# State sums of a Mamba block taken time-major: accumulating transposes, the skip term as a matmul, gated rows turned back in pairs

## The chip, the cores and the metric

The kernel runs on one core of a Trainium2 chip. The metric is the device time of one execution in microseconds (us). The kernel before was run three times: 1104.54 us median, 1101.55 to 1105.68. A further, profiled execution took 1106.44 us.

## What is computed

A decoder layer on x of 8 batches of 256 positions and 256 channels: a Mamba block (selective scan), cross attention with a feed-forward part, and a mixture of 160 experts, each behind a layer norm. The change lies in the Mamba block, whose end the reference writes so:

```
u = silu(conv(x_in)); dt, Bm, Cm = split(u @ x_proj_w.T)
delta = softplus(dt @ dt_proj_w.T + dt_proj_b)
h = h * exp(delta_t * A) + (delta_t * u_t) * b_t      # for each channel d and state n
y = einsum('bdn,bn->bd', h, c_t)                      # sum over 16 states
y = ys + u * D_param
y = y * silu(z)
out = y @ out_proj_w.T
```

There are 512 inner channels d, 16 states n and 256 time steps t per batch.

## The kernel before

Everything is float32 but for a few masks. Five engine programs, written out by hand, run side by side and meet by semaphores; the order of each engine's work is the order of the calls in its function `turn(s, p)`. Turn s works on four batches at once: the scan of batch s, the attention front of batch s-1, the feed-forward part of s-2, routing of s-3 and its scatter to DRAM (also of s-4), and the projections of batch s+1. Ten turns (-2 to 7), then a hand-made tail that finishes the last batches. Behind this front, which ends near 750 us, come the experts and a combining stage, which the change doesn't touch.

**The scan.** The 512 channels are 4 chunks c of 128 partitions, the 16 states 4 groups of 4. One of the 16 steps t of a batch takes one group and one chunk: ScalarE makes the decays in a PSUM tile DA (two of them; `decay`, L722 and four exponentials L725), GpSimd makes the inflow (three buffers; `inflow`, L462), VectorE scans (`scan`, L1668, 128x1024) and multiplies by C into one of four SBUF tiles hb (`outflow`, L1675). TensorE adds the four states of hb into the PSUM bank Y (`sum_`, L1123): four matmuls with the identity as weights and 256 columns of hb moving, so that Y holds channel by time. `inflow(t)` waits for scan t-2 to start and scan t-3 to end; `decay(t)` waits for outflow t-2.

**The gate.** After four steps a chunk is complete, and VectorE does `y(b, p, c)`: L1681 adds u * D to Y in PSUM, L1684 multiplies by silu(z) and writes the result over u. The four calls stand in VectorE's list after scan 5 (c = 0), scan 10 (c = 1), before scan 13 (c = 2), and after scan 1 of the next turn (c = 3). The first sum of the next chunk waits for `y` (y_d), since it overwrites Y. `out_proj` (L1135) takes the gated u as weights. It needs all four chunks and stands in the next turn, in bank QA.

**Around it.** `in_proj(b, 2)` and `in_proj(b, 3)` (L1087) make z, channel by time, copied to `sz` by ScalarE (`z_in`, L674). `conv_` (L1096) and `conv_out` (L667) are the convolution through bank PB and its bias. On VectorE the moments of a layer norm end in L1698; the root that GpSimd takes of them is L468 to L473 (`ln_root`). `ln0` follows scan 4, `ln1` stands just before y of c = 2. `router` on TensorE (L1248) is read by VectorE in L1741 at the head of the next turn. `acc` takes the shared expert's result (`shared_out`, L1753) and is stored to DRAM; `base2` (L499, GpSimd, `base2_`) is the feed-forward's residual, and GpSimd reaches it after `inflow` 5. In the tail, `out7(c)` (L1453) is the output projection of the last batch, and `ffn1_6` (L1549) stands between its pieces.

Of the kernel before, what the change touches and what calls it, by code (L numbers as in the profile page):

```python
# [80 lines left out]
def decoder_kernel(nc, a, out):  # L81
    ctx = ExitStack()
    with ctx:
# [24 lines left out]
        b_dt = sb("b_dt", [P, NC])  # L108
        a_neg = sb("a_neg", [P, NC, NS])
# [43 lines left out]
        k_scaled = sig("k_scaled")  # L153
# [21 lines left out]
        y_du = sig("y_du", NC)  # L175
# [64 lines left out]
        acc = sb("acc", [P, QT, D])  # L240
# [35 lines left out]
        full, used = xin[:, 0, 0:NE], xin[:, 1, 0:1]  # L276

# [151 lines left out]
        def front_gpsimd(pool):  # L429
# [65 lines left out]
            def base2_(b):  # L495
                pool.wait_ge(aff1_d.sem, aff1_d.at(b, 2))
                if ff_c.at(b - 1, 1, True):
                    pool.wait_ge(ff_c.sem, ff_c.at(b - 1, 1))
                g.tensor_tensor(base2[:, :, :], x2a[:, :, :], row(B2), ALU.add).then_inc(aff1_d.sem, 1)  # L499
# [150 lines left out]
        def front_scalar(act):  # L650
# [19 lines left out]
            def z_in(b, p, f):  # L670
                if f == 0 and y_d.at(b - 2, NC, True):
                    act.wait_ge(y_d.sem, y_d.at(b - 2, NC))
                act.wait_ge(proj_f.sem, proj_f.at(b, f + 5))
                s.activation(sz[p][:, 2 * f:2 * f + 2, :], pair(PB), ACT.Copy).then_inc(proj_c.sem, 1)  # L674
# [38 lines left out]
            def decay(b, p, t):  # L713
                gr, c = t % NG, t // NG
                if t == 0:
                    act.wait_ge(dl_d.sem, dl_d.at(b, 1))
                    if isinstance(b, int) and b == 0:
                        act.wait_ge(k_scaled.sem, 2)
# [91 lines left out]
            def first_batch():  # L810
                FB = [PB, QA]
                for f in range(2):
                    act.wait_ge(proj_f.sem, f + 1)
                    s.activation(xin[:, 2 * f:2 * f + 2, TAPS - 1:], pair(FB[f]), ACT.Copy).then_inc(proj_c.sem, 1)
                for f in range(2):
                    act.wait_ge(proj_f.sem, f + 3)
                    for i in range(2):
                        c = 2 * f + i
                        ins = s.activation(du[0][:, c, :], pair(FB[f])[:, i, :], ACT.Identity, bias=b_conv[:, c:c + 1])
                    ins.then_inc(proj_c.sem, 1)  # L820
                    act.wait_ge(proj_c.sem, f + 3)
# [18 lines left out]
                s.activation(sz[0][:, :, :], sz[0][:, :, :], ACT.Silu).then_inc(gate_d.sem, 1)  # L840

            first_batch()
            def turn(s, p):
# [5 lines left out]
                if exists(s + 1) and s >= 0:  # L849
                    conv_out(s + 1, 1 - p, 1)  # L850
                if exists(s) and s > 0:
                    decay(s, p, 3)
# [66 lines left out]
                if exists(s + 2) and s > -2:  # L919
                    x_in(s + 2, 0)  # L920
                if s == -1:
# [102 lines left out]
            def tail():  # L1024
                chosen_exp(L5)
                last_eps()
# [43 lines left out]
        def front_tensor(pe):  # L1070
            mm, tr = nc.tensor.matmul, nc.tensor.transpose

            def in_proj(b, f):
# [10 lines left out]
                for i in range(2):  # L1084
                    c = 2 * f + i
                    for k in range(KD):
                        ins = mm(pair(PB)[:, i, :], w_in[:, k, c * P:(c + 1) * P], xt[:, k, :],  # L1087
                                 start=k == 0, stop=k == KD - 1)
# [26 lines left out]

            def sum_(b, t):
                gr, c = t % NG, t // NG
                if gr == 0:
                    if y_d.at(b, c, True):
                        pe.wait_ge(y_d.sem, y_d.at(b, c))  # L1120
                pe.wait_ge(outflow_d.sem, outflow_d.at(b, t + 1))
                for n in range(SG):
                    ins = mm(Y[:, 0:T], ident[:, :], hb[t % NH][:, n, :],  # L1123
                             start=gr == 0 and n == 0, stop=gr == NG - 1 and n == SG - 1, skip_group_check=True)
                ins.then_inc(sum_d.sem, 1)

            def out_proj(b, p):
                pe.wait_ge(y_d.sem, y_d.at(b, NC))
                if acc_d.at(b - 2, 1, True):
                    pe.wait_ge(acc_d.sem, acc_d.at(b - 2, 1))  # L1130
                elif mg_c.at(b - 1, 1, True):
                    pe.wait_ge(mg_c.sem, mg_c.at(b - 1, 1))
# [107 lines left out]
            def x2T(b, p):  # L1240
                pe.wait_ge(norm_d[3].sem, norm_d[3].at(b, 1))
                turned(x2[p], QF, x2T_f)
# [70 lines left out]
            def first_batch():  # L1313
# [32 lines left out]
                for f in range(2):  # L1346
                    pe.wait_ge(proj_c.sem, f + 5)
                    projected(FB[1 - f], f + 2)

            first_batch()  # L1350
            def turn(s, p):
# [10 lines left out]
                if exists(s - 3):  # L1362
                    rank(s - 3)
                if exists(s):
                    sum_(s, 0)
                if exists(s - 1):
# [3 lines left out]
                if exists(s):  # L1370
                    sum_(s, 1)
# [12 lines left out]
                if exists(s):  # L1384
                    sum_(s, 4)
# [35 lines left out]
                if exists(s):  # L1421
                    sum_(s, 8)
# [12 lines left out]
                if exists(s):  # L1435
                    sum_(s, 12)
# [146 lines left out]
            def tail():  # L1583
# [5 lines left out]
                ffn1_6(0)  # L1589
                out7(2)  # L1590
# [43 lines left out]
        def front_vector(dve):  # L1634
# [10 lines left out]
            v.tensor_scalar(a_neg[:, :, :], a_neg[:, :, :], -1.0, None, ALU.mult).then_inc(k_scaled.sem, 2)  # L1645
# [934 lines left out]
```

## Time and profile before

| | us |
|---|---|
| profiled execution | 1106.44 |
| its span | 1104.7 |
| median of three runs | 1104.54 |
| TensorE busy (matmul) | 955.0 (86%) |
| VectorE busy | 838.1 (76%) |
| GpSimd busy | 746.9 (68%) |
| ScalarE busy | 631.5 (57%) |
| first scan of batch 0 starts | 43.07 |
| last step (outflow) of batch 7 starts | 652.43 |
| first matmul of the experts | 757.11 |

PE is TensorE's matmuls, PEld its weight loads, DVE VectorE, ACT ScalarE, POOL GpSimd, SP the engine that issues most transfers. L12 is line 12 of the kernel before. Busy time is what instructions cover; the shares are means over stages that differ, so the table alone doesn't say what bounds the scan. A matmul of float32 shows as two instructions in the trace where the program has one; a transpose shows as one.

### The profile page before, as it was taken

The page shows a single profiled execution, that of the slowest core. Times are in us where ns is not written, and L with a number is a line of the kernel's source. Part 1 is how long each engine was busy: PE and PEld are TensorE (multiplying, and loading weights), DVE is VectorE, ACT ScalarE, POOL GpSimd, SP SyncE. Part 2 cuts the span into 40 slices and gives each one's busy share as a digit, 9 for nine tenths or more (in the row PEclk, how much of TensorE's full clock was granted, in tenths as well). Part 3 has the DMA queues.
Part 4 walks back from the last instruction along what each step waited for, and adds up shares of the span by engine and source line. Part 5 has one row for each costly group of instructions (what it writes and reads, how often), then busy time and mean ns, then how long its engine had stood idle before and what let it go on. Part 6 is the DMA issues. An engine that isn't in the chain of part 4 may idle for free. (4 is left out here: it accounts for less than half of the span.)

```text
span 1104.7 us, 17544 instructions
## 1 busy us (share of the span) xinstructions
PE 955.0 (86%) x4878; PEld 799.0 (72%) x4878; DVE 838.1 (76%) x1640; ACT 631.5 (57%) x1560; POOL 746.9 (68%) x648
## 2 busy tenths in 40 slices
PE   6698979999999999999988989705999899999386
PEld 4476758788888888888866877605878787788264
DVE  0669999999999999999999984663655555555277
ACT  4776686785875876866855543403645455555200
POOL 1444585757679889888988886563777777777500
PEclk9698999999999999999989989967999999999799
DMA  7472764835115224224143112438998989988486
GB/s 241 172 244 91 233 197 153 262 106 172 41 35 179 77 64 150 72 96 142 39 142 96 43 61 74 160 111 273 328 305 261 293 287 284 295 277 258 157 341 265
DMA packets 118252, 195.46 MB, mean 177 GB/s; under 512 B 17476, under 2 KB 83170, under 8 KB 115714
## 3 DMA queue, kind: packets, MB, share of 16 engines
q1 hardware_dynamic: 79682, 134.54, 37.8%
q0 software_dynamic: 16512, 35.19, 8.7%
q10 hardware_dynamic: 21952, 24.51, 6.9%
q8 instruction: 42, 0.69, 0.3%
q14 instruction: 64, 0.52, 0.2%
HBM read 155.21 MB, written 75.64 MB: 209 GB/s over the span
## 5 line engine op out<-in xcount | busy, mean ns | idle before, releaser
L462 POOL TENSOR_TENSOR inf_all<-bc_all,du 128x1024 f32<-128x1024 f32 x128 | 300.6, 2367 | 97.0 <-DVEq L1666 48.5
L1668 DVE TENSOR_TENSOR_SCAN DA<-DA,inf_all 128x1024 f32<-128x1024 f32 x128 | 293.1, 2290 | 15.6 <-ACT DA L725 12.7
L2223 POOL DMA_INDIRECT yp_dram<-u,sz x216 | 212.9, 986 | 79.3 <-issue 41.7
L1123 PE MATMUL Y<-hb_all,ident 128*128 128x256 f32 x1024 | 247.3, 389 | 12.5 <-DVE u L1684 12.5
L1123 PEld LDWEIGHTS Y<-hb_all,ident 128*128 128x128 f32 x1024 | 197.2, 195 | 44.8 <-DVE u L1684 16.4
L725 ACT ACTIVATE DA<-dl,a_neg 128x255 f32<-128x255 f32 x512 | 211.9, 461 | 0.2
L2290 ACT ACTIVATE u<-DA,sz 128x256 f32<-128x256 f32 x216 | 102.6, 475 | 112.6 <-DMA yp_dram<-u,sz 79.6
L1675 DVE TENSOR_TENSOR hb_all<-DA,bc_all 128x1024 f32<-128x1024 f32 x128 | 155.8, 1218 | 8.2 <-DVE DA L1668 1.0
L2258 PE MATMUL DA<-hb_all,sz 128*128 128x256 f32 x432 | 136.6, 398 | 18.8 <-ACT sz L2283 17.7
L2251 PE MATMUL DA<-sz,hb_all 128*128 128x128 f32 x864 | 132.9, 277 | 2.9 <-issue 2.9
L2251 PEld LDWEIGHTS DA<-sz,hb_all 128*128 128x128 f32 x864 | 114.3, 193 | 3.7 <-issue 3.3
L2390 DVE COPY sz<-QA 128x256 f32<-128x256 f32 x108 | 45.8, 424 | 89.4 <-PE QA L2242 86.1
L515 POOL DMA_INDIRECT xe_dram<-x2e,ad_i x80 | 86.3, 1078 | 18.3 <-issue 17.1
L2258 PEld LDWEIGHTS DA<-hb_all,sz 128*128 128x128 f32 x432 | 65.5, 191 | 30.0 <-ACT sz L2283 28.4
L722 ACT ACTIVATE DA<-zeros 128x4 f32<-128x4 f32 x128 | 22.4, 175 | 104.3 <-DVE hb_all L1675 101.4
L2283 ACT ACTIVATE sz<-DA 128x128 f32<-128x128 f32 x216 | 59.1, 273 | 36.2 <-PE DA L2251 24.5
L1087 PE MATMUL PB<-xt,w_in 128*128 128x256 f32 x224 | 57.5, 402 | 16.8 <-DMA xt<-in_xT 9.5
L2242 PE MATMUL PB<-ident,inf_all 128*128 128x128 f32 x216 | 41.8, 276 | 34.8 <-DMA inf_all<-xe_dram 34.8
L2390 DVE COPY sz<-PB 128x256 f32<-128x256 f32 x108 | 45.8, 424 | 25.8 <-PE PB L2242 25.3
L2242 PEld LDWEIGHTS PB<-ident,inf_all 128*128 128x128 f32 x216 | 30.7, 143 | 45.8 <-DMA inf_all<-xe_dram 35.2
L1087 PEld LDWEIGHTS PB<-xt,w_in 128*128 128x128 f32 x224 | 43.8, 200 | 27.2 <-DMA xt<-in_xT 9.9
L1096 PE MATMUL PB<-xin,w_tap 128*128 128x256 f32 x224 | 51.1, 380 | 2.7 <-ACT du L667 2.0
(460 smaller groups left out, 1589.3 us busy)
## 6 DMA issues: line engine op xcount, KB each, us to landing
hb_all<-in_w_moe SPq DMA_DIRECT2D x216, 256.0 KB
bc_all<-bc_dram SPq DMA_DIRECT2D x32, 1024.0 KB, 5.9
inf_all<-xe_dram SPq DMA_DIRECT2D x216, 140.0 KB
bc_all<-yp_dram SPq DMA_DIRECT2D x16, 1024.0 KB, 6.9
xe_dram<-zeros ACTq DMA_DIRECT2D x2, 7420.0 KB, 26.0
xe_dram<-zeros ACTq DMA_DIRECT2D x1, 7560.0 KB, 27.1
yp_dram<-u,sz POOLq DMA_INDIRECT x216
xt<-in_xT SPq DMA_DIRECT2D x8, 256.0 KB, 5.8
```

What stands on the lines that cost most here:

```text
L462: g.tensor_tensor(inf[(b * NTAU + t) % NI][:, :, :], bc[gr][:, 0, :, :], du[p][:, c, :].unsqueeze(1).to_broadcast([P, SG, T]), ALU.mult).t ...
L515: g.indirect_dma_start(xe_dram, bass.IndirectOffsetOnAxis(ap=ad_i[b % 2][:, q, k:k + 1], axis=0), x2e[p][:, q, :].bitcast(I32), None).then ...
L725: ins = s.activation(da[:, n, 1:T], dl[p][:, c, 1:T], ACT.Exp, scale=a_neg[:, c, st:st + 1])
L1087: ins = mm(pair(PB)[:, i, :], w_in[:, k, c * P:(c + 1) * P], xt[:, k, :], start=k == 0, stop=k == KD - 1)
L1123: ins = mm(Y[:, 0:T], ident[:, :], hb[t % NH][:, n, :], start=gr == 0 and n == 0, stop=gr == NG - 1 and n == SG - 1, skip_group_check=True)
L1668: v.tensor_tensor_scan(da[:, :], da[:, :], inf[(b * NTAU + t) % NI][:, :, :].rearrange("p n t -> p (n t)"), 0.0, ALU.mult, ALU.add).then_i ...
L1675: v.tensor_tensor(hb[t % NH][:, :, :], states(DA[t % NDA]), bc[t % NG][:, 1, :, :], ALU.mult).then_inc(outflow_d.sem, 1)
L2223: g.indirect_dma_start(yp_dram, bass.IndirectOffsetOnAxis(ap=pid[:, half * UNROLL + s_:half * UNROLL + s_ + 1], axis=0), ys[s_][:, :], Non ...
L2251: ins = mm(UP[s_ % 2][:, 0:P], wt[s_][:, k * INTER:(k + 1) * INTER], xgT[s_ % 2][:, k, :], start=k == 0, stop=k == KD - 1)
L2258: mm(DN[s_ % 2][:, 0:D], h1[s_ % 2][:, :], wt[s_][:, KD * INTER:], start=True, stop=True).then_inc(dn_f.sem, 1)
L2290: s.activation(ys[s_][:, :], DN[s_ % 2][:, 0:D], ACT.Identity, scale=both[:, s_, 0:1]).then_inc(dn_c.sem, 1)
L2390: v.tensor_copy(xgT[s_ % 2][:, :, :], XT[s_ % 2][:, 0:KD * P].rearrange("p (k t) -> p k t", k=KD)).then_inc(xgT_c.sem, 1)
```

## The change

TensorE now builds Y time-major: two quarters of 128 time steps, each 128 partitions (time) by 128 columns (channels).

- `sum_`: each state of hb is the weights of two 128x128 transposes, with the identity moving, that accumulate in Y. Eight transposes take the place of four matmuls.
- `skip_`, new: u * D comes from two matmuls per chunk, u as weights and `d_tap` (a diagonal matrix of D, made once on ScalarE by four ACTIVATEs) moving. It opens the chunk's sum and has the wait for `y` of the chunk before.
- `y`: L1681 is gone. One VectorE multiply takes Y times silu(z) and writes over sz.
- z is projected time-major: two matmuls with 512 columns instead of four with 256, of the same columns in all.
- The gated rows have to be channel-major for `out_proj`. `gated_turned`, new, turns two chunks (four transposes), and `gated_out`, new, copies them from PSUM to u on ScalarE (128x512). Half 0 goes through bank QF late in the turn, half 1 through QA early in the next.
- `acc` and `base2` share one tile; `base2_` waits for the store of acc of the batch before. Sum 1 is moved ahead of `out_proj`.

```
 def in_proj(b, f):
...
+    else:
+        for k in range(KD):
+            ins = mm(PB[:, :], xt[:, k, rows_half(f - 2)], w_in[:, k, DI:], start=k == 0, stop=k == KD - 1)
+def skip_(b, p, c):
+    if y_d.at(b, c, True):
+        pe.wait_ge(y_d.sem, y_d.at(b, c))
+    else:
+        pe.wait_ge(a_exp.sem, 2)
+    for q in range(QT):
+        mm(YT[:, q, :], u[p][:, c, rows_half(q)], d_tap[:, c, :], start=q == 0, stop=False, skip_group_check=True)
 def sum_(b, t):
...
     for n in range(SG):
-        ins = mm(Y[:, 0:T], ident[:, :], hb[t % NH][:, n, :],
-                 start=gr == 0 and n == 0, stop=gr == NG - 1 and n == SG - 1, skip_group_check=True)
+        for q in range(QT):
+            ins = mm(YT[:, q, :], hb[t % NH][:, n, rows_half(q)], ident[:, :], is_transpose=True,
+                     start=False, stop=gr == NG - 1 and n == SG - 1, skip_group_check=True)
+def gated_turned(b, p, half, bank):
...
+    for i in range(2):
+        c = 2 * half + i
+        for q in range(QT):
+            ins = tr(pair(bank)[:, i, rows_half(q)], gated[p][:, q, c * P:(c + 1) * P], ident[:, :])
+    ins.then_inc(gT_f.sem, 1)
 def out_proj(b, p):
-    pe.wait_ge(y_d.sem, y_d.at(b, NC))
...
+    pe.wait_ge(gT_c.sem, gT_c.at(b, 2))
+def gated_out(b, p, half, bank):
+    act.wait_ge(gT_f.sem, gT_f.at(b, half + 1))
+    s.activation(u[p][:, 2 * half:2 * half + 2, :], pair(bank), ACT.Copy).then_inc(gT_c.sem, 1)
 def y(b, p, c):
     dve.wait_ge(gate_d.sem, gate_d.at(b, 1))
     dve.wait_ge(sum_d.sem, sum_d.at(b, NG * (c + 1)))
-    v.scalar_tensor_tensor(Y[:, 0:T], u[p][:, c, :], d_par[:, c:c + 1], Y[:, 0:T],
-                           ALU.mult, ALU.add).then_inc(y_du.sem, 1)
-    dve.wait_ge(y_du.sem, y_du.at(b, c + 1))
-    v.tensor_tensor(u[p][:, c, :], Y[:, 0:T], sz[p][:, c, :], ALU.mult).then_inc(y_d.sem, 1)
+    at = slice(c * P, (c + 1) * P)
+    v.tensor_tensor(gated[p][:, :, at], YT, gated[p][:, :, at], ALU.mult).then_inc(y_d.sem, 1)
 first_batch (ScalarE)
+    for c in range(NC):
+        ins = s.activation(d_tap[:, c, :], ident[:, :], ACT.Copy, scale=d_par[:, c:c + 1])
 tail (TensorE)
     ffn1_6(0)
+    gated_turned(L7, 1, 1, DA1[0])
     out7(2)
```

TensorE's list at the head of a steady turn, before (hs, ws_d: shared expert; w_tap: convolution; msk_b, m_sum: routing; w_out: output projection):

```order
L1264 MATMUL QA<-ws_d,hs 128x256 x2
L1096 MATMUL PB<-xin,w_tap 128x256 x8
L1123 MATMUL Y<-hb_all,ident 128x256 x4
L1087 MATMUL PB<-xt,w_in 128x256 x4
L1271 MATMUL QF<-msk_b,earlier 128x160
L1272 MATMUL QF<-m_sum,ones 128x160
L1273 MATMUL QF<-msk_b,earlier 128x160
L1274 MATMUL QF<-msk_b,ones 128x160
L1275 MATMUL QF<-m_sum,ones 128x160
L1123 MATMUL Y<-hb_all,ident 128x256 x4
L1135 MATMUL QA<-w_out,u 128x256 x8
L1087 MATMUL PB<-xt,w_in 128x256 x4
```

The same place in the changed kernel (L1151 the transposing sums, L1172 the turning back, L1144 the skip term):

```order
L1118 MATMUL PB<-xin,w_tap 128x256 x8
L1151 MATMUL Y<-ident,hb_all 128x128 x8
L1110 MATMUL PB<-w_in,xt 128x512 x2
L1316 MATMUL QF<-msk_b,earlier 128x160
L1317 MATMUL QF<-m_sum,ones 128x160
L1318 MATMUL QF<-msk_b,earlier 128x160
L1319 MATMUL QF<-msk_b,ones 128x160
L1320 MATMUL QF<-m_sum,ones 128x160
L1172 MATMUL QA<-ident,sz 128x128 x4
L1144 MATMUL Y<-d_tap,u 128x128 x2
L1151 MATMUL Y<-ident,hb_all 128x128 x16
L1179 MATMUL QA<-w_out,u 128x256 x8
```

The turning back and the skip term stand ahead of sums 0 and 1, and both sums ahead of the output projection.

ScalarE's list at the same place, before (L786 is the routing mask, L667 conv_out, then decay 3, z, decay 4):

```order
L786 ACTIVATE msk_b<-rep,m_half 128x320
L667 ACTIVATE du<-PB,b_conv 128x256 x2
L722 ACTIVATE DA<-zeros 128x4
L725 ACTIVATE DA<-dl,a_neg 128x255 x4
L674 ACTIVATE sz<-PB 128x512
```

and in the changed kernel:

```order
L796 ACTIVATE msk_b<-rep,m_half 128x320
L673 ACTIVATE du<-PB,b_conv 128x256 x2
L736 ACTIVATE u<-QA 128x512
L728 ACTIVATE DA<-zeros 128x4
L731 ACTIVATE DA<-dl,a_neg 128x255 x4
L680 ACTIVATE sz<-PB 128x512
```

The copy of half 1, L736, now stands between the convolution's bias and decay 3. The copy of half 0 stands in the same way between an x copy and decay 14.

## Rows read from the trace of the kernel before

**Rows 1.** Engines' busy time in two stretches; last columns clock, DMA share, GB/s.
```profile
100.00:280.00 180.00, 169.25 (x771) 140.95 (x770) 169.03 (x156) 123.23 (x294) 115.99 (x77) 0.99 0.56 178
280.00:550.00 270.00, 267.43 (x1255) 224.82 (x1254) 263.04 (x334) 200.90 (x470) 229.11 (x182) 1.00 0.28 92
```
**Rows 2.** VectorE's timeline: start, us covered; scan 6 of two turns, one y.
```profile
373.25 2.30 DVE L1668 TENSOR_TENSOR_SCAN DA<-DA,inf_all 128x1024 f32<-128x1024 f32 x1
...
429.48 0.47 DVE L1681 SCALAR_TENSOR_TENSOR Y<-u,d_par,Y 128x256 f32<-128x256 f32 x1
429.98 0.42 DVE L1684 TENSOR_TENSOR u<-Y,sz 128x256 f32<-128x256 f32 x1
...
451.78 2.30 DVE L1668 TENSOR_TENSOR_SCAN DA<-DA,inf_all 128x1024 f32<-128x1024 f32 x1
```
**Rows 3.** VectorE's waits from 100 to 280 us, and one in its timeline.
```profile
DVE DA L1668 <- ACT DA L725: 4.5, 6, 1.0
...
106.43 0.49 DVE L1681 SCALAR_TENSOR_TENSOR Y<-u,d_par,Y 128x256 f32<-128x256 f32 x1 [1.70 <-PE Y L1123]
```
**Rows 4.** TensorE's timeline: a sum's matmuls, four transposes, the next sum.
```profile
438.49 1.89 PE L1123 MATMUL Y<-hb_all,ident 128*128 128x256 f32 x8
440.22 0.60 PE L1141 MATMUL QF<-ident,x2a 128*128 128x128 f32 x4
440.66 1.89 PE L1123 MATMUL Y<-hb_all,ident 128*128 128x256 f32 x8
```
**Rows 5.** Timelines of GpSimd and VectorE: root, inflows and scans 14 and 10.
```profile
409.96 0.25 DVE L1698 BATCH_NORM_AGGREGATE mv<-stats 128x2 f32<-128x6 f32 x2
410.41 0.22 POOL L468 TENSOR_SCALAR ve<-mv 128x2 f32<-128x2 f32 x1 [0.22 <-DVE mv L1698]
411.95 6.99 POOL L462 TENSOR_TENSOR inf_all<-bc_all,du 128x1024 f32<-128x1024 f32 x3
414.50 2.29 DVE L1668 TENSOR_TENSOR_SCAN DA<-DA,inf_all 128x1024 f32<-128x1024 f32 x1
...
385.09 2.37 POOL L462 TENSOR_TENSOR inf_all<-bc_all,du 128x1024 f32<-128x1024 f32 x1
387.77 2.29 DVE L1668 TENSOR_TENSOR_SCAN DA<-DA,inf_all 128x1024 f32<-128x1024 f32 x1
```
**Rows 6.** Timelines around decay 3 and scan 3 of turn 5.
```profile
429.37 1.99 PE L1087 MATMUL PB<-xt,w_in 128*128 128x256 f32 x8 [0.61 <-ACT du L667]
431.54 1.93 PE L1123 MATMUL Y<-hb_all,ident 128*128 128x256 f32 x8
431.57 0.18 ACT L722 ACTIVATE DA<-zeros 128x4 f32<-128x4 f32 x1 [2.26 <-DVE hb_all L1675]
431.68 1.65 ACT L725 ACTIVATE DA<-dl,a_neg 128x255 f32<-128x255 f32 x4
434.99 2.29 DVE L1668 TENSOR_TENSOR_SCAN DA<-DA,inf_all 128x1024 f32<-128x1024 f32 x1
```
**Rows 7.** Two ScalarE lines' instructions: ns min/median/max, first and last start.
```profile
L730 ACT ACTIVATE qT<-QA x7: 579/580/598, 165.0 to 626.0; 128x512 f32<-128x512 f32 x7
L807 ACT ACTIVATE w_tap<-ident,w_conv x16: 385/386/387, 7.6 to 11.9; 128x128 f32<-128x128 f32 x16
```
**Rows 8.** TensorE's timeline: out7(2) of the tail.
```profile
658.31 1.89 PE L1453 MATMUL DA<-w_out,u 128*128 128x256 f32 x8
```
**Rows 9.** DMA issues: the store of acc, KB, us to landing.
```profile
acc_dram<-acc SPq DMA_DIRECT2D x8, 256.0 KB, 3.4
```
**Rows 10.** TensorE after a long wait, and the window (columns as rows 1).
```profile
642.68 3.78 PE L1123 MATMUL Y<-hb_all,ident 128*128 128x256 f32 x8 [3.78 <-DVE u L1684]
...
641.90:648.80 6.90, 6.12 (x17) 4.96 (x18) 6.42 (x5) 4.46 (x10) 6.36 (x8) 0.51 0.04 14
```
**Rows 11.** Timelines: the router's matmuls, and VectorE reading them.
```profile
419.64 1.25 PE L1248 MATMUL QF<-w_r,fT 128*128 128x160 f32 x8
421.58 0.48 DVE L1741 TENSOR_TENSOR key<-QF,b_r 128x320 f32<-128x320 f32 x1
```

More of the change, by code:

```diff
@@ L108, in decoder_kernel @@
         b_dt = sb("b_dt", [P, NC])
+        d_tap = sb("d_tap", [P, NC, P])
         a_neg = sb("a_neg", [P, NC, NS])
@@ L239, in decoder_kernel @@
         hs = sb("hs", [P, T])
-        acc = sb("acc", [P, QT, D])
+        acc = base2
         stats = sb("stats", [P, 4, QT, 6])
@@ L276, in decoder_kernel @@
         full, used = xin[:, 0, 0:NE], xin[:, 1, 0:1]
+        YT = Y[:, 0:T].rearrange("p (q d) -> p q d", q=QT)
+        gated = [t[:, :, :].rearrange("p c t -> p (c t)").rearrange("p (q d) -> p q d", q=QT) for t in sz]
         def pair(bank):
@@ L498, in base2_ @@
                     pool.wait_ge(ff_c.sem, ff_c.at(b - 1, 1))
+                if b < L6 and acc_st.at(b - 1, 16, True):
+                    pool.wait_ge(acc_st.sem, acc_st.at(b - 1, 16))
+                pool.sem_inc(tick, 1)
                 g.tensor_tensor(base2[:, :, :], x2a[:, :, :], row(B2), ALU.add).then_inc(aff1_d.sem, 1)
@@ L670, in z_in @@
             def z_in(b, p, f):
-                if f == 0 and y_d.at(b - 2, NC, True):
-                    act.wait_ge(y_d.sem, y_d.at(b - 2, NC))
+                if f == 0 and gT_f.at(b - 2, 2, True):
+                    act.wait_ge(gT_f.sem, gT_f.at(b - 2, 2))
                 act.wait_ge(proj_f.sem, proj_f.at(b, f + 5))
@@ L850, in turn @@
                     conv_out(s + 1, 1 - p, 1)
+                if exists(s - 1):
+                    gated_out(s - 1, 1 - p, 1, QA)
                 if exists(s) and s > 0:
@@ L920, in turn @@
                     x_in(s + 2, 0)
+                if exists(s):
+                    gated_out(s, p, 0, QF)
                 if s == -1:
@@ L1083, in in_proj @@
                     pe.wait_ge(proj_c.sem, proj_c.at(b, f if f < 2 else f + 2))
-                for i in range(2):
-                    c = 2 * f + i
+                if f < 2:
+                    for i in range(2):
+                        c = 2 * f + i
+                        for k in range(KD):
+                            ins = mm(pair(PB)[:, i, :], w_in[:, k, c * P:(c + 1) * P], xt[:, k, :],
+                                     start=k == 0, stop=k == KD - 1)
+                else:
                     for k in range(KD):
-                        ins = mm(pair(PB)[:, i, :], w_in[:, k, c * P:(c + 1) * P], xt[:, k, :],
-                                 start=k == 0, stop=k == KD - 1)
+                        ins = mm(PB[:, :], xt[:, k, rows_half(f - 2)], w_in[:, k, DI:], start=k == 0, stop=k == KD - 1)
                 ins.then_inc(proj_f.sem, 1)
@@ L1125, in sum_ @@
                 ins.then_inc(sum_d.sem, 1)
-            def out_proj(b, p):
-                pe.wait_ge(y_d.sem, y_d.at(b, NC))
[L1129 to L1132, printed above, removed]
+            def gated_turned(b, p, half, bank):
+                if half == 0:
+                    pe.wait_ge(y_d.sem, y_d.at(b, 2))
+                    if ff_c.at(b - 2, 1, True):
+                        pe.wait_ge(ff_c.sem, ff_c.at(b - 2, 1))
+                elif b == L7:
+                    pe.wait_ge(y_d.sem, y_d.at(L7, NC))
+                    pe.wait_ge(outflow_d.sem, outflow_d.at(L7, NTAU))
+                else:
+                    pe.wait_ge(y_d.sem, y_d.at(b, NC))
+                    if acc_d.at(b - 2, 1, True):
+                        pe.wait_ge(acc_d.sem, acc_d.at(b - 2, 1))
+                    elif mg_c.at(b - 1, 1, True):
+                        pe.wait_ge(mg_c.sem, mg_c.at(b - 1, 1))
+                for i in range(2):
+                    c = 2 * half + i
+                    for q in range(QT):
+                        ins = tr(pair(bank)[:, i, rows_half(q)], gated[p][:, q, c * P:(c + 1) * P], ident[:, :])
+                ins.then_inc(gT_f.sem, 1)
@@ L1347, in first_batch @@
                     pe.wait_ge(proj_c.sem, f + 5)
-                    projected(FB[1 - f], f + 2)
+                    for k in range(KD):
+                        ins = mm(FB[1 - f][:, :], xt[:, k, rows_half(f)], w_in[:, k, DI:], start=k == 0, stop=k == KD - 1)
+                    ins.then_inc(proj_f.sem, 1)
             first_batch()
@@ L1363, in turn @@
                     rank(s - 3)
+                if exists(s - 1):
+                    gated_turned(s - 1, 1 - p, 1, QA)
                 if exists(s):
+                    skip_(s, p, 0)
                     sum_(s, 0)
+                    sum_(s, 1)
                 if exists(s - 1):
@@ L1384, in turn @@
                 if exists(s):
+                    skip_(s, p, 1)
                     sum_(s, 4)
@@ L1421, in turn @@
                 if exists(s):
+                    skip_(s, p, 2)
                     sum_(s, 8)
@@ L1435, in turn @@
                 if exists(s):
+                    gated_turned(s, p, 0, QF)
+                    skip_(s, p, 3)
                     sum_(s, 12)
```

17 lines of the change are left out of this document (7 added, 10 removed).

## The prediction

> **What bounds the kernel now.** I read first the busy time by stretch. From 280 to 550 us VectorE is covered for 263.0 of 270 us and TensorE for 267.4 [rows 1]: both look full, so one has to be asked who waits. The list of waits for VectorE in that stretch is empty, and its timeline runs back to back from scan 6 of one turn to scan 6 of the next, 451.78 - 373.25 = 78.5 us [rows 2]. TensorE is full too, but late rather than decisive: nothing on VectorE stands waiting for it. So a steady turn lasts as long as VectorE's list, and what comes off that list comes off the turn, until GpSimd, ScalarE or TensorE is in the way. From 100 to 280 us VectorE is covered for 169.0 of 180 us, and there its list of waits has entries: 4.5 us on ScalarE's decays in six places [rows 3]. Profiled, the kernel took 1106.44 us for a span of 1104.7; the median of its runs is 1104.54, 1.9 us less. I sum against the profiled execution and take the difference off the median. A measurement of this kernel tells some 0.5% (5.5 us) from no change; that is where "same" ends below.
>
> **VectorE.** L1681 goes. From its start to that of L1684 is 429.98 - 429.48 = 0.50 us [rows 2], 32 times. The multiply that stays has the same 128x256 elements, PSUM and SBUF in, SBUF out: I keep its 0.42. Of the 32, four free nothing: c = 0 of turns 0 and 2, where scan 6 comes after a decay that ScalarE has not finished, and c = 2 and c = 3 of batch 7, behind which the tail hangs on other work. So 28 x 0.50 = **14.0 us**.
>
> **TensorE.** Eight instructions of 256 columns for one sum cover 1.89 us, the next work begins 440.22 - 438.49 = 1.73 after [rows 4]: 0.216 each. Four transposes start at 440.22 and the next work at 440.66 [rows 4], so one takes 0.44/4 = 0.11. Eight take 0.87 where 1.73 stood: 16 x 0.86 = 13.8 us less per turn. The skip term is eight ordinary matmuls of 128 columns per turn, 16 instructions at half of 0.216: 1.7 us more. Turning back is eight transposes, 0.9. The z projection streams the same columns. Net 11.2 us less per turn. Nothing of this counts directly, since VectorE didn't wait for it in a steady turn. It counts where waits on TensorE, or on ScalarE held up by TensorE, showed: 1.7 us before y of c = 2 in turn 0 [rows 3], and of the 4.5 us of late decays about 3.0, as ScalarE had stood there waiting for transposes, queries and scores. I leave 1.5 of the 4.5, where ScalarE's own list of table loads and gates is full. **4.7 us** in all.
>
> **What takes back.** *GpSimd.* Between the end of the moments (L1698, 410.21) and scan 14 (414.50) VectorE has y of c = 2, scan 13 and outflow 13; GpSimd has the root and inflow 14, which ends at 411.95 + 6.99/3 = 414.28, and with some 0.07 of signalling is 0.15 ahead [rows 5]. Of 0.50 only 0.15 can be had: 0.35 lost in turns 1 to 6, 2.1 us. In the same way inflow 10 ends at 387.46 for a scan at 387.77 [rows 5], behind a GpSimd list that runs without a wait from the root of ln0 on; of c = 0's 0.50, 0.25 is lost in the four turns with both batches' scatters, 1.0 us. *ScalarE.* The half-1 copy stands before decay 3. in_proj ends and the next work starts at 431.54 [rows 6]; that is where turning back now stands: 0.60, then the copy, 0.58 [rows 7], with signals until 432.75; decay 3 is 431.57 to 433.33, so 1.76 long, and ends at 434.5. Scan 3 starts at 434.99 now, 434.49 with y shortened [rows 6]. It just fits; for turns 1 and 2, whose VectorE list is shorter there, I put 0.3 each and 0.3 for the rest, 0.9 us. The half-0 copy stands before decay 14, which by the timeline has some 4 us to spare: nothing, covered by y, scan 13 and outflow 13; without that cover it would cost its 0.58 and TensorE's 0.60. *d_tap* is four ACTIVATEs on ScalarE's path of the first turn, (11.9 - 7.6)/15 = 0.29 apart [rows 7], 1.1 us, ahead of the first x copy, on which TensorE's first projections wait. *Order.* in_proj 3 of turn 0 comes 0.3 later, behind sum 1 and the skip. *Tail.* out7(2) and (3) start at 658.31 behind ffn1_6 [rows 8]; before them sum 15 is 0.86 shorter, and turning back 0.60, copy 0.58 and two signals come between: 0.5 later. *acc in base2's tile.* GpSimd now waits for a store of 3.4 us [rows 9] issued in the head of the turn, with four inflows of 2.3 us between: nothing; were it late, inflow 6 behind it and the scan would wait. Sum: 2.1 + 1.0 + 0.9 + 1.1 + 0.3 + 0.5 = **5.9 us**.
>
> **The sum** is 14.0 + 4.7 - 5.9 = 12.8 us: 1093.6 for the profiled execution, **1091.7** against the median.
>
> **TensorE's clock.** TensorE will now idle some 10 us a turn. In turn 7 it stood 3.78 us for y of c = 2, and the next eight instructions took 3.78 instead of 1.89; the granted clock was 0.51 from 641.9 to 648.8 [rows 10], 1.2 GHz instead of 2.4. So a long wait costs half of some 7 us, 3.4. In the changed kernel TensorE reaches that wait about 3 us early in every turn. No row shows a long run of transposes, so what they do to the clock is open. The Trainium skill ("TensorE: Matmul & The Clock Gate", "Part 4: PE-mode transpose") says that transpose mode does not count as TensorE being busy in the way a matmul does. By it the low clock would come more often than with the matmuls of before, and the second rival below would be the likelier case; the transposes in the trace stand singly between matmuls at 1.00, which neither confirms nor excludes it.
>
> **Rivals.**
> 1. *Nothing takes back* (0.17). GpSimd and ScalarE keep ahead, as their lists have waits elsewhere: 32 x 0.50 + 4.7 = 20.7, 1083.8 us. Against it: the 0.15 and 0.31 us of rows 5.
> 2. *A low clock after the wait for y of c = 2, each turn* (0.22). From there to the router TensorE loses 3.4, gets back 2 x 0.86 for sums 12 and 13, pays 0.44 for the skip: 2.1 late. The router ends at 420.89 and is read at 421.58 [rows 11], 0.7 later: a stall of 1.4 in turns 3 to 7, 7 us. 1098.7 us. Bounds are 0 and 3.4 per turn.
> 3. *A low clock in in_proj at the head of the turn* (0.11). The 1.73 us ahead of turning back double; decay 3 and scan 3 are late by 1.7, seven times 12.1: 1103.8 us, no change. It decides when TensorE idles about 3.8 us before that place; before, it idled 0.61 [rows 6].
> 4. *Slower: the low clock from the convolution to the copy* (0.05). Same place, but the stretch of 6.9 us starts earlier, so the whole 3.4 lands between VectorE's y of c = 3 and decay 3, in series: 7 x 3.4 = 23.8 on top of the forecast, 1115.5 us. It decides when that place loses over 1.8 us per turn.
> 5. *The accumulating transposes don't run as transposes* (0.03). Each goes in two steps, eight take 1.73 again, and with 2.6 us added TensorE's turn is 77.8 + 2.6 = 80.4, longer than 78.5: 7 x 1.9 = 13.3 slower than before, 1117.8 us. The order of instructions marks them as single ones of 128 columns, but that list has ordinary float32 matmuls as single too.
>
> **Numbers.** The forecast has 0.42, the larger gain 0.17, rivals 2 to 5 0.22, 0.11, 0.05 and 0.03. Faster by over 0.5% means below 1099.0: the first three, less a little of rival 2: 0.79. Same 0.13, slower 0.08. The range leaves out rivals 4 and 5 and the far ends of 1 and 3: 1084.5 to 1103.5.
>
> **What would show it.** Steady turns of 76.5 to 77.3 us from scan 6 to scan 6, VectorE waiting for inflow 14 (about 0.35) and inflow 10. Sums of eight transposes covering about 1.03. TensorE's busy share in the steady stretch near 88%, with idle time before the skip of c = 3. Scan 3 without a wait on ScalarE over 0.3. Wrong if a sum shows 16 instructions, if the granted clock there is under 0.9 and the router or y waits appear, if the multiply takes over 0.5, or if turns stay at 78.

## The result and the profile after

The changed kernel takes 1098.03 us (median of 12 runs, 1095.76 to 1101.17) against 1105.24 for the kernel before in the same session: ratio 0.9932, 95% interval 0.9917 to 0.9948. By the ratio that is 7.5 us faster (6 to 9), where 12.8 were forecast. The profiled execution took 1096.14 us, its span 1094.4. The profiled executions lie 10.3 us apart, and 2.7 of these stand behind the last scan (454.7 us before, 452.0 after). The profiles of the runs below, but for a_warm, scatter there from 450.6 to 455.7, so only the scan stages are compared from here on.

The steady stretch in the changed kernel, as engines' busy time (TensorE, its weight loads, VectorE, ScalarE, GpSimd; then clock, DMA share, GB/s), against [rows 1]:

```profile
100.00:280.00 180.00, 152.00 (x837) 124.90 (x836) 169.50 (x155) 129.03 (x309) 115.94 (x78) 0.97 0.57 180
280.00:550.00 270.00, 243.07 (x1331) 201.52 (x1330) 261.85 (x317) 205.07 (x482) 232.89 (x183) 0.98 0.27 91
```

TensorE came down by 24 us in the second stretch, to 90% (forecast: near 88%). VectorE, which lost an instruction some 14 times there, is covered as before. The starts of scan 6 in VectorE's timeline tell where the gain lies, against [rows 2]:

```profile
366.33 2.30 DVE L1722 TENSOR_TENSOR_SCAN DA<-DA,inf_all 128x1024 f32<-128x1024 f32 x1
...
444.71 2.30 DVE L1722 TENSOR_TENSOR_SCAN DA<-DA,inf_all 128x1024 f32<-128x1024 f32 x1
```

444.71 - 366.33 = 78.4 us, where the kernel before has 78.5 and I expected 76.5 to 77.3. From scan 6 of batch 0 to scan 6 of batch 3 the three first turns take 214.8 us instead of 220.9; the four turns behind them 78.37 each instead of 78.57. So 6.1 us of the gain are from the early turns and 0.8 from the four steady ones. The steady turns are not alike: one by one they take 77.56, 78.38, 78.73 and 78.79 us, where the kernel before has 78.52 to 78.63.

**Where the 2.0 us of a steady turn went.** Measured from the start of one VectorE instruction to the start of the next, the turn above loses the four L1681 (0.50, 0.49, 0.50, 0.52) and 0.13 just ahead of y of c = 0, 2.14 in all. These grow: the softplus combination, a SCALAR_TENSOR_TENSOR behind scan 11 (L1650, now L1704), by 0.52; the time up to scan 14 by 0.47; the time up to y of c = 3 by 0.22; up to scan 3 (behind a late decay) by 0.16; and the cast of the expert numbers from integer to float at the end of routing (L1774, now L1826) by 0.67, 2.04 in all. Some 0.1 us are left. The list of VectorE's waits shows one of the five entries:

```profile
DVE DA L1722 <- POOL inf_all L465: 1.1, 3, 0.4
DVE hb_all L1729 <- DVE DA L1722: 0.5, 1, 0.5
```

The first is inflow 14, which was forecast at 0.35. The second is one pause ahead of an outflow in turn 5; what it waits for isn't shown, and the kernel before has the same once, in turn 7. The two largest entries are not waits in the profile's sense but longer instructions. Before the change, in VectorE's and GpSimd's timelines (the two inflows of L462 end at 444.51 + 4.68 = 449.19, the one cast at 449.22):

```profile
444.51 4.68 POOL L462 TENSOR_TENSOR inf_all<-bc_all,du 128x1024 f32<-128x1024 f32 x2
...
448.82 0.40 DVE L1774 CAST x2e<-ti 128x16 f32<-128x16 uint32 x1
```

and after it (inflows until 442.11, cast until 442.13):

```profile
437.44 4.67 POOL L465 TENSOR_TENSOR inf_all<-bc_all,du 128x1024 f32<-128x1024 f32 x2
...
441.06 1.07 DVE L1826 CAST x2e<-ti 128x16 f32<-128x16 uint32 x1
442.05 0.16 DVE L1828 TENSOR_SCALAR pr<-pr 128x16 f32<-128x16 f32 x1
```

The cast begins earlier and ends when GpSimd's inflow ends. In all ten turns of both traces that have an inflow beside it, it ends 0.02 to 0.04 us behind the inflow; in the tail, with GpSimd elsewhere, the same cast takes 0.17. The softplus combination shows the same (first before, then after; GpSimd's three inflows end at 395.66 and 388.73):

```profile
388.65 7.01 POOL L462 TENSOR_TENSOR inf_all<-bc_all,du 128x1024 f32<-128x1024 f32 x3
...
395.47 1.27 DVE L1650 SCALAR_TENSOR_TENSOR th<-xin,th 128x1024 f32<-128x1024 f32 x1
```
```profile
381.72 7.01 POOL L465 TENSOR_TENSOR inf_all<-bc_all,du 128x1024 f32<-128x1024 f32 x3
388.89 1.81 POOL L521 DMA_INDIRECT xe_dram<-x2e,ad_i  x1 [0.17 <-issue]
394.20 0.23 POOL L471 TENSOR_SCALAR ve<-mv 128x2 f32<-128x2 f32 x1 [3.50 <-DVE mv L1750]
...
388.03 1.78 DVE L1704 SCALAR_TENSOR_TENSOR th<-xin,th 128x1024 f32<-128x1024 f32 x1
```

It takes 1.22 us in turns without an inflow beside it, and in the others ends 1.08 to 1.10 after the inflow, whenever it started. These are hidden waits: time in which an instruction has been started and stands, with no idle time in the profile.

The Trainium skill ("SBUF — State Buffer", section "Who interferes with whom") has a mechanism for it: VectorE and GpSimd share one pair of SBUF ports; a VectorE instruction with two SBUF inputs contends with a GpSimd instruction that reads SBUF, and so does a copy, a cast or a tensor_scalar in a two-port mode, where whoever issues first keeps the pair for its whole instruction and the other is blocked. The traces agree as far as they go, with the numbers above; they show the ends that keep together, not the ports.

### The profile page after: what moved, and what is told of

Read it like the earlier page. It is cut to its first block and busy times, and to the rows that moved or that the text cites. A ratio compares the mean times of both kernels' runs of the same rounds, so it can differ in the third digit from the quotient of the medians.

```text
span 1094.4 us, 17775 instructions
## 1 busy us (share of the span) xinstructions
PE 881.8 (81%) x5006; PEld 734.5 (67%) x5006; DVE 828.1 (76%) x1608; ACT 638.1 (58%) x1580; POOL 746.1 (68%) x648
## 5 line engine op out<-in xcount | busy, mean ns | idle before, releaser
L2342 ACT ACTIVATE u<-DA,sz 128x256 f32<-128x256 f32 x216 | 102.5, 475 | 109.9 <-DMA yp_dram<-u,sz 76.9
L1151 PE MATMUL Y<-ident,hb_all 128*128 128x128 f32 x1024 | 132.6, 279 | 0.8 <-DVE hb_all L1729 0.8
L1151 PEld LDWEIGHTS Y<-ident,hb_all 128*128 128x128 f32 x1024 | 121.0, 145 | 8.9 <-issue 2.6
L1118 PE MATMUL PB<-xin,w_tap 128*128 128x256 f32 x224 | 53.4, 392 | 6.5 <-ACT xin L665 3.7
L1118 PEld LDWEIGHTS PB<-xin,w_tap 128*128 128x128 f32 x224 | 43.2, 196 | 14.7 <-ACT xin L665 4.7
L1106 PE MATMUL PB<-xt,w_in 128*128 128x256 f32 x112 | 31.6, 432 | 25.2 <-DVE vv L1742 12.4
```

What stands on the lines that cost most here:

```text
L1118: ins = mm(pair(PB)[:, i, :], w_tap[:, c * TAPS + k, :], xin[:, c, k:k + T], start=k == 0, stop=k == TAPS - 1)
L1151: ins = mm(YT[:, q, :], hb[t % NH][:, n, rows_half(q)], ident[:, :], is_transpose=True, start=False, stop=gr == NG - 1 and n == SG - 1, sk ...
L2342: s.activation(ys[s_][:, :], DN[s_ % 2][:, 0:D], ACT.Identity, scale=both[:, s_, 0:1]).then_inc(dn_c.sem, 1)
```

## The experiments

The expectations speak of three theories. V is the forecast: VectorE's list alone sets the turn. G says that GpSimd's chain does, through the hidden waits; G2 and G3 are later forms of it. C says that TensorE's low clock took the gain back.

Turn lengths (scan 6 to scan 6, us, from VectorE's timeline in one profiled execution each) and ratios to the kernel before, measured beside each run. Two of the profiled executions are far from their kernel's median: a_p4's was its fastest, 6.1 us below, and b_pool's its slowest, 5.0 us above. Ratios whose intervals overlap don't tell two kernels apart.

| kernel | first three turns | next four, mean | ratio (95%) |
|---|---|---|---|
| before | 220.9 | 78.57 | 1 |
| changed | 214.8 | 78.37 | 0.9932 (0.9917-0.9948) |
| b_nostt | 216.4 | 78.33 | 0.9951 (0.9931-0.9971) |
| a_stt | 218.6 | 78.62 | 0.9972 (0.9956-0.9987) |
| a_pool | 213.0 | 78.34 | 0.9933 (0.9913-0.9953) |
| b_pool | 224.6 | 78.71 | 1.0005 (0.9986-1.0024) |
| a_p4 | 213.5 | 77.62 | 0.9918 (0.9894-0.9943) |
| a_p3 | 214.8 | 78.43 | 0.9964 (0.9943-0.9985) |
| b_p4 | 220.7 | 78.70 | 0.9997 (0.9978-1.0016) |
| a_p5 | 213.3 | 77.85 | 0.9901 (0.9879-0.9923) |
| a_p6 | 213.0 | 76.88 | 0.9892 (0.9868-0.9916) |
| bn_p6 | 215.4 | 78.67 | 0.9975 (0.9946-1.0003) |

**The two halves of the change apart.**

```
 b_nostt: def y (before)
-                v.scalar_tensor_tensor(Y[:, 0:T], u[p][:, c, :], d_par[:, c:c + 1], Y[:, 0:T], ALU.mult, ALU.add)
 a_stt: def y (changed)
+                v.scalar_tensor_tensor(Y[:, 0:T], u[p][:, c, :], zeros[:, 0:1], Y[:, 0:T], ALU.mult, ALU.add)
```

> The kernel before with L1681 taken out and nothing else (the skip term u*D is left out of the result). It takes 32 x 0.50 us off VectorE's list and leaves TensorE as it was. Theory G (GpSimd's chain sets the steady turn, and VectorE waits for it inside two of its own instructions, the softplus combination and the cast of the expert numbers, which the profile shows as long instructions and not as idle time): both instructions grow, from 1.27 to about 1.78 and from 0.40 to about 1.07 us, scan 14 waits about 0.35, and only the 0.50 of y of c = 3 and some 0.15 of c = 2 are kept: steady turns of 77.8 to 78.0 us, 4 to 6 us faster in all. Theory V (my forecast: VectorE's list alone, less the inflows): turns of 76.8 to 77.0, 10 to 12 us faster. Theory C (the gain is there, but TensorE's clock took it back in the changed kernel): here TensorE is busy as before, so all of 14 us less 3 would show, as with V.

> The changed kernel with an operation of L1681's size (128x256, PSUM and SBUF in, PSUM out, with a scalar of zero, so that nothing changes in the result) put back on VectorE ahead of the multiply: the change on TensorE alone. Theory G: of the 4 x 0.50 us per turn those of c = 0 and c = 1 fall into the waits inside the cast and the softplus combination (which shrink to 0.4 to 0.5 and 1.25 to 1.3 us), that of c = 2 mostly into the wait for inflow 14: turns of 78.9 to 79.3 from turn 3 on, the kernel 3 to 6 us slower than the changed kernel, so 1 to 4 us faster than before. Theory V: 14 us slower than the changed kernel, 5 to 7 slower than before.

VectorE's half alone is worth 5.4 us, TensorE's half alone 3.1; together they give 7.5 (5.4 and 7.5 are not told apart by their intervals). Theory V wanted 10 to 12 us for the first and a loss of 5 to 7 for the second, and falls. In a_stt cast and softplus combination shrink to 0.52 to 0.56 and 1.26 to 1.28 us, nearly as G had it, but the turns are 78.62, not 78.9 to 79.3. And in b_nostt G has the amount and not the reason: cast and softplus combination did not grow (0.40 and 1.22, but for one cast of 1.08 in turn 7), the turns are 78.33, not 77.8 to 78.0, and what VectorE waits for is another engine:

```profile
DVE DA L1668 <- ACT DA L725: 3.4, 4, 0.9
DVE u L1681 <- PE Y L1123: 2.2, 4, 0.6
DVE DA L1668 <- POOL inf_all L462: 1.1, 3, 0.4
```

TensorE is busy 267.3 of 270 us in it, as before, and y of c = 0 waits for its sum. I had called TensorE "late rather than decisive"; it was 0.2 us a turn from deciding. The wait for ScalarE stands at scan 11 and seems to come from TensorE too: ScalarE stands up to 0.9 us a turn for TensorE's L1113 some 4 us ahead of that decay, and in the changed kernel, with more work on ScalarE, it doesn't. So TensorE's relief is needed for VectorE's to count, and in the changed kernel it is there.

**GpSimd's order, first try.** In a_pool and b_pool inflow 6 stands ahead of the root of the first norm, inflow 14 between two roots, scatter 5 behind inflow 0:

```
-                    ln_root(s - 1, 0)
                     inflow(s, p, 6)
+                    ln_root(s - 1, 0)
                     inflow(s, p, 7)
...
-                    scatter(s - 3, 1 - p, 5)
                     ln_root(s - 2, 3)
+                    inflow(s, p, 14)
                     ln_root(s - 1, 1)
-                    inflow(s, p, 14)
                     inflow(s, p, 15)
                     inflow(s + 1, 1 - p, 0)
+                    scatter(s - 3, 1 - p, 5)
```

> The changed kernel with GpSimd's list in another order, same work: inflow 6 ahead of the root of the first norm, inflow 14 between the roots of the fourth and the second norm, and one scatter moved from ahead of them to behind inflow 0. Theory G: the cast is back at 0.2 us, the softplus combination at 1.22, no wait at scan 14: turns of 76.9 to 77.3, 6 to 9 us faster than the changed kernel, about 1090 us. Theory C (TensorE's low clock and late copies took the gain): no change, within 2 us.

> The kernel before with the same new order of GpSimd's list. Theory G: VectorE's list is full there, and the hidden waits are small (0.22 of the cast, 0.05 to 0.15 of the softplus combination): turns of 78.2 to 78.3, 1 to 2 us faster than before. If the new order were good or bad by itself, for the scatters or the router, it would show here: 6 us or more either way.

A miss for G as it stood: no wait at scan 14 any more, but in two turns 0.42 and 0.68 us of idle time appeared ahead of scan 2, the cast grew to 1.39 to 1.43 us in three, and the softplus combination stayed at 1.78 to 1.89. The order had only moved the wait. In the kernel before, the ratio shows no change; the 1 to 2 us that were expected lie at the edge of its interval.

**Which part of GpSimd's list.** a_p3 moves scatters 4 and 5 ahead of the third norm's root, into GpSimd's 3.50 us of idle time in the rows above. a_p4 has this and the two inflow moves of a_pool; b_p4 is a_p4's order in the kernel before.

> The changed kernel with three moves in GpSimd's list: scatters 4 and 5 ahead of the third norm's root, where GpSimd stands idle for 3.5 us in every turn; inflow 6 ahead of the first norm's root; inflow 14 between the roots of the fourth and the second norm. Theory G2 (a loop through VectorE and GpSimd sets the turn: inflow 13 ends, the softplus combination may run, 5.5 us later VectorE has the third norm's moments, and from that root GpSimd works with hardly a gap to the next inflow 13; moving work within the gapless part, as a_pool did, can only shift the wait, filling the 3.5 us shortens the loop by 2.5): softplus combination back at 1.22 us, cast at 0.17 to 0.5, no wait at scan 14, turns of 76.6 to 77.6, 4 to 8 us faster than the changed kernel. Theory C (TensorE's low clock and the copy hold the turn at 78.4): no change.

> Of the three moves only that of scatters 4 and 5 into the gap. Theory G2: the softplus combination at 1.22 us, so 0.5 us of the turn; the cast still ends with the inflow before it (the stretch between the first norm's moments and that inflow is untouched) and scan 14 still waits 0.4: turns of 77.7 to 78.2, 2 to 4 us faster than the changed kernel. Theory C: no change.

> The three moves in the kernel before. There VectorE (78.5) and TensorE (78.3, as the run without L1681 showed) hold the turn at the same length, so GpSimd's relief gives at most 0.2 us a turn: 0 to 2 us faster than before. If it is 4 us or more, GpSimd was the bound before too, and the loop is older than the change.

a_p3 misses: the softplus combination still takes 1.81 to 1.88 us, and the kernel is no faster than the changed one. a_p4's turns are 0.75 us shorter in its profile, at the low end of what was expected, and its ratio can't be told from the changed kernel's. b_p4 came as expected: no change. What a_p3 and a_p4 leave as it was is the time from the end of inflow 7 (the cast) to the end of inflow 13 (the softplus combination), 25.0 us in the changed kernel and in a_p4, in which GpSimd has hardly a gap: an earlier cast and an earlier list start move together. That is theory G3.

**Is the long cast a wait?**

```
 a_cast: def weigh (semaphore waits left out)
-                v.tensor_copy(rows_[:, :, E0:E0 + TOPK], ti[:, :, :])
                 v.tensor_scalar(pr[:, :, :], pr[:, :, :], 1.0, None, ALU.add)
...
                 v.tensor_tensor(rows_[:, :, G0:G0 + TOPK], pr[:, :, :], psm...)
+                v.tensor_copy(rows_[:, :, E0:E0 + TOPK], ti[:, :, :])
```

> The changed kernel with the cast of the expert numbers moved behind the product at L1840, so that TENSOR_SCALAR of pr comes first at that place. If the long cast is a wait for a path that GpSimd's inflow holds, then the instruction that now stands there takes over the wait: TENSOR_SCALAR of pr 0.9 to 1.1 us instead of 0.16 and ending within 0.05 us of the inflow's end, the cast 0.17, the kernel within 2 us of the changed one. If the cast is long by itself (its types), it stays at 1.07 in its new place and TENSOR_SCALAR at 0.16.

One profiled execution, 1095.84 us. The place keeps its wait and the instruction doesn't (the inflows end at 438.23 + 4.67 = 442.90):

```profile
438.23 4.67 POOL L465 TENSOR_TENSOR inf_all<-bc_all,du 128x1024 f32<-128x1024 f32 x2
...
441.87 1.07 DVE L1827 TENSOR_SCALAR pr<-pr 128x16 f32<-128x16 f32 x1
442.97 0.25 DVE L1829 RECIPROCAL pr<-pr 128x16 f32<-128x16 f32 x1
...
443.95 0.17 DVE L1841 CAST x2e<-ti 128x16 f32<-128x16 uint32 x1
```

In all five turns TENSOR_SCALAR takes 1.06 to 1.08 us and the cast 0.17.

**The refined order, and TensorE's clock.**

```
 a_p5 (with inflow 6 and 14 as in a_p4, scatter 5 behind inflow 0)
-                    scatter(s - 4, p, 8)
                     inflow(s, p, 2)
+                    scatter(s - 4, p, 8)
...
-                    scatter(s - 3, 1 - p, 2)
                     inflow(s, p, 10)
...
                     inflow(s, p, 13)
+                    scatter(s - 3, 1 - p, 2)
                     scatter(s - 3, 1 - p, 3)
+                    scatter(s - 3, 1 - p, 4)
                     ln_root(s - 2, 2)
 a_warm (TensorE)
+                    fill(4)
                     shared_out(s - 3)
...
+                    fill(6)
                     in_proj(s + 2, 0)
 a_warm: def in_proj
-                    for i in range(2):
+                    for i in (0, 1, 0, 1)[:2 + 2 * f]:
```

fill(n) is n products of 256 columns into the upper half of Y's bank. The last edit makes the products of in_proj 1 twice.

> The changed kernel with all of GpSimd's gapless stretches shortened: as in a_p4 (inflow 6 ahead of the first norm's root, inflow 14 between two roots), and scatter 2 taken out from ahead of inflow 10 (with 3 and 4 it now fills the 3.5 us gap behind inflow 13), scatter 5 behind inflow 0, scatter 8 behind inflow 2. Theory G3: what counts is GpSimd's time between two meetings with VectorE, and from the end of inflow 7 (the cast) to that of inflow 13 (the softplus combination) it has no gap, 24.7 us; only taking a scatter (1.3 us) out of it frees the second meeting, which a_p3 did not do. Softplus combination 1.22 us, cast 0.17 to 0.5, no wait at scan 14 and at scan 3: turns of 76.3 to 77.2, 8 to 11 us faster than the changed kernel over the whole front, 1087 to 1091 us. If TensorE's clock and the copies are what stands behind GpSimd (theory C), turns stay above 77.6 and waits on ScalarE or TensorE appear at scan 3 and y of c = 3.

> The changed kernel with TensorE kept at work in its three long waits of a turn: six products of 256 columns that nobody reads ahead of in_proj 0, in_proj 1 done twice, four such products ahead of the shared expert's output, 5.2 us a turn in all. Theory C: the low-clock stretches of 3.4 us at the head of turns 4 to 6 go, y of c = 3 waits no more, turns 0.3 to 0.6 us shorter, 2 to 3 us in all. Theory G3: the low-clock stretches go, y of c = 3 comes 0.2 earlier and the turn stays at 78.3 to 78.7, because the cast ends with the inflow whatever comes before it: within 1.5 us of the changed kernel.

a_p5: the softplus combination is at 1.22 us in every turn, as G3 had it, and scan 14 waits no more. But the cast takes 1.41 to 1.42 in three turns of five, scan 3 waits 0.42 and 0.67 us for its inflow in two, and the turns are 77.85, no shorter than a_p4's and longer than the 76.3 to 77.2 expected: the cast, which ends with inflow 7 at the head of the turn, had become the late meeting:

```profile
437.72 1.41 DVE L1825 CAST x2e<-ti 128x16 f32<-128x16 uint32 x1
...
463.39 1.22 DVE L1703 SCALAR_TENSOR_TENSOR th<-xin,th 128x1024 f32<-128x1024 f32 x1
```

a_warm's products write to the bank in which Y is being summed, and it computes something else than the changed kernel; which of its edits does that no run separates. Its stages behind the last scan take 463.5 us instead of 452.0, so its total, 1.0099 (1.0072 to 1.0127), says nothing, and only the front is read. The low-clock stretch at the head of turn 5 is gone and y of c = 3 there is on time; the stretch from scan 6 of turn 4 to that of turn 5 takes 78.33 us instead of 78.38, since the cast still ends with its inflow (1.07). The first three turns take 222.0 instead of 214.8; that the added products stood in the way there is argued, not shown. The good reading is of one turn only, as the next got longer by 1.1; that C is not needed, a_p6 tells more plainly.

**The order that fits, with and without TensorE's relief.** a_p6 is a_p5 with scatter 1 too in the gap behind inflow 13, scatters 5 and 6 ahead of the fourth norm's root, scatter 7 ahead of inflow 1, scatter 11 behind inflow 7. bn_p6 is b_nostt with this order.

> The changed kernel with a further order of GpSimd's list: a_p5, and besides scatter 1 into the gap behind inflow 13 (2.28 us idle were left there), scatters 5 and 6 into the gap ahead of the fourth norm's root (3.06 us idle), scatter 7 ahead of inflow 1, scatter 11 behind inflow 7. The head of the turn, whose end is the cast (1.42 us long in a_p5), has 3.8 us less to do. Theory G3: cast 0.17 to 0.5, softplus combination 1.22 to 1.5, no waits for inflows: turns of 76.5 to 77.2 (VectorE's own list is 78.5 less 2.0), 1 to 6 us faster than a_p5, 8 to 11 faster than the changed kernel. If turns stay at 77.8, something that is not GpSimd's order holds them.

> The kernel before with L1681 taken out (as b_nostt: the skip term is left out) and with the same order of GpSimd's list as a_p6: VectorE and GpSimd relieved, TensorE not. In b_nostt the waits were on TensorE (y of c = 0, 0.6 us a turn) and on ScalarE behind it (0.8), with TensorE busy 267 of 270 us. If TensorE's list of some 78.3 us a turn is a bound of its own, turns stay at 78.2 to 78.4 and the kernel within 2 us of b_nostt. If GpSimd alone is the bound, turns fall to 76.5 to 77.2 as in a_p6, 6 us faster than b_nostt, and TensorE's saving in the change was worth nothing in steady turns.

a_p6 has turns of 76.17, 76.15, 76.82 and 78.39 (the last one holds a wait of 2.31 us for the router at the head of turn 7, behind 18 us, 549 to 567, in which the granted clock was 0.62): 0.9892, the lowest ratio of all, 11.9 us under the kernel before; a_p5's interval overlaps it, the changed kernel's doesn't, by a hair. Cast and softplus combination in its turn 4:

```profile
436.89 0.17 DVE L1825 CAST x2e<-ti 128x16 f32<-128x16 uint32 x1
...
461.34 1.22 DVE L1703 SCALAR_TENSOR_TENSOR th<-xin,th 128x1024 f32<-128x1024 f32 x1
```

bn_p6 has the same two at 0.17 and 1.22 and still turns of 78.38, 78.26, 78.28 and 79.76 (the last with 2.49 us for the router), for TensorE is full (busy time as above, VectorE third, then VectorE's waits):

```profile
280.00:550.00 270.00, 267.20 (x1258) 226.31 (x1257) 256.88 (x316) 203.09 (x472) 230.68 (x183) 1.00 0.28 91
```
```profile
DVE DA L1667 <- ACT DA L724: 3.6, 4, 0.9
DVE u L1680 <- PE Y L1122: 1.9, 4, 0.6
DVE key L1737 <- PE QF L1247: 1.0, 3, 0.4
```

So the turn of the kernel before stood on three engines at once: VectorE's list 78.5 us (its timeline), TensorE's 78.3 (bn_p6, the other two relieved), and GpSimd's stretches between their meetings with VectorE 78.4 (the changed kernel, the other two relieved). The change took 2 us off the first; of the second it took 7.9 us of busy time a turn (77.7 to 69.8 in turn 4), and 9.9 in a_p6's turn 4, where the clock was at 1.00 throughout. With GpSimd relieved as well most of the 2 us appear: 76.2 in two turns, 76.9 on average. No run relieves TensorE and GpSimd and leaves VectorE's list; that it would stay at 78.5 is argued from its timeline without idle time.

## Why the forecast came out as it did

The direction was right and 7.5 us lie inside the range of 1.0 to 20.0 us; of the 12.8 us forecast, little more than half came. That the number came so near is in part luck: by its own sign of being wrong, "turns stay at 78", the mechanism failed, and the gain is nearly all from the three early turns, where VectorE's part came in full and the relieved waits, to which the forecast gave as much again, did not.

*VectorE, 28 x 0.50 = 14.0 us.* This is the step that failed, with the reading under it that nobody waits, since the timeline "runs back to back". Two waits for GpSimd's inflow stood inside instructions, and the cast had 0.23 us of one before the change already (0.40 instead of 0.17). In four steady turns 0.8 us came in place of 8, or of 5.6 after the 0.35 and 0.25 a turn that GpSimd was to take back. The multiply that stays takes 0.41 us, as taken.

*Waits of the early turns, 4.7 us.* This term failed as well. The wait ahead of y of c = 2 in turn 0 came down from 1.70 to 0.83 and did not go, and scan 14 behind it now waits 0.63 for its decay. Late decays still cost VectorE 4.8 us from 100 to 280 us, against the 4.5 of [rows 3]:

```profile
DVE DA L1722 <- ACT DA L731: 4.8, 7, 1.4
DVE sz L1736 <- PE Y L1151: 0.8, 1, 0.8
```

The three turns still gave 6.1 us (2.1, 1.5 and 2.5), which is VectorE's 2.0 a turn and next to nothing of the waits. Two waits on ScalarE in turn 2 went (1.0 and 0.5), but others came, among them 1.0 at scan 9 of turn 1. The 2.0 a turn counts there because the cast is in the list from turn 3 on only, and the softplus combination is stretched from turn 4 on only. Whether TensorE's clock kept the rest isn't shown: from 43 to 280 us it was 0.94 on average, 0.96 before.

*TensorE, -11.2 us a turn, not counted directly.* Its prices hold: eight transposes cover 1.04 and the next work starts 0.88 after; the skip term takes 0.44 from start to start where TensorE comes to it without a wait (0.55 in the row below, behind one); turning back covers 0.60. The busy time of the turn fell by less, 7.9 and 9.9 us as told above:

```profile
398.77 1.04 PE L1151 MATMUL Y<-ident,hb_all 128*128 128x128 f32 x8
399.65 1.98 PE L1106 MATMUL PB<-xt,w_in 128*128 128x256 f32 x8
401.46 0.60 PE L1172 MATMUL QF<-ident,sz 128*128 128x128 f32 x4
403.65 0.71 PE L1144 MATMUL Y<-d_tap,u 128*128 128x128 f32 x4 [1.59 <-DVE sz L1736]
```

But "Nothing of this counts directly" is wrong in the sense that bn_p6 shows: without it TensorE bounds the turn at 78.3. Rival 5 (transposes in two steps) is out: a sum has 8 instructions. a_stt gives the whole half 3.1 us, 1.4 to 4.9.

*What takes back, 5.9 us.* Inflow 14: 0.39, forecast 0.35 [rows 5]. The 0.07 of signalling in that sum stands in no row; each scan that waits for its inflow starts 0.13 behind the inflow's end, in both kernels, and with it the forecast would have been 0.41. Inflow 10: nothing, forecast 0.25. The copy ahead of decay 3: 0.16 us a turn, forecast to just fit [rows 6]. d_tap: 1.26 us on ScalarE, forecast 1.1. The tail: from the last scan to the experts' first matmul it is 107.1 us before and 105.8 after, forecast 0.5 longer, but the profiles of all runs scatter there from 105.1 to 109.0. What was missing is the 0.52 and 0.67 of the two hidden waits, about 1.2 us a turn.

*TensorE's clock, rivals 2 to 4.* The granted clock fell in three stretches of 3.4 us between 280 and 550 us: late in turn 3, behind a wait of 2.7 us for VectorE's v, and at the heads of turns 5 and 6, behind waits of 2.0 and 2.4 us for the shared expert's hs. The one in turn 5, with the columns of the busy time, against the 6.9 us of [rows 10]:

```profile
415.70:419.10 3.40, 3.40 (x9) 2.70 (x9) 3.40 (x3) 0.80 (x3) 3.18 (x3) 0.50 0.94 347
```

It fell on the convolution, not on the router, and y of c = 3 behind it was 0.2 us late. The router was read late once, by 0.76 us in turn 7, at the end of 18 us (555 to 573) in which the granted clock was 0.53. So something like rival 2's mechanism exists, at a tenth of its price, and a_p6 pays 2.31 us for it in the same place; the others did not show. The rule on transpose mode that the prediction weighed stays open: each of the three stretches begins behind a wait, so they don't separate the two. Nor does every wait bring one: in turn 4 TensorE stood 3.3 us for the same v, and the clock stayed at 1.00.

## What to carry to other kernels

An engine whose timeline has no idle time can still be waiting: compare the same instruction's duration across turns and in the tail, and where one is longer see whether its end, not its start, keeps a fixed distance to another engine's end. Before an instruction is taken off a full engine, look for the second and third engine at the same length; here three stood within 0.3 us of 78.5, and of the runs only the one that relieved all three came near the 2 us. And a list of in-order work with idle time has room only in its gap: moving work within the gapless stretch moves the wait (a_pool). Moving it into the gap shortens the turn only where it comes out of the stretch that sets it (a_p6), not else (a_p3).

## What the runs showed of the hardware

A cast of 128x16 elements that takes 0.17 us takes up to 1.43 us beside GpSimd's 128x1024 product and ends 0.02 to 0.04 us behind it; a TENSOR_SCALAR of the same size takes 1.06 to 1.08 instead of 0.16 in the same place, and a SCALAR_TENSOR_TENSOR of two SBUF inputs ends 1.08 to 1.10 us behind the product. GpSimd's own instructions get longer too: the scatter beside that instruction and the next takes 1.80 or 1.81 us in the changed kernel, the one beside VectorE's du<-dl,u 1.87 or 1.88, and the others from 280 to 620 us 0.96 to 1.20; that VectorE holds them is argued from the place alone. Transposes that accumulate in PSUM run at 0.11 us per 128x128 block, as those that don't accumulate did [rows 4].
